# Routed experts on tiles of gathered rows in place of all experts on all tokens, in an attention and mixture-of-experts block

## What is computed

```python
logits = x @ gate_w.T                       # E = 8 experts
_, idx = top_k(logits + lb_bias, 2)         # two experts for each token
w = sigmoid(logits at idx); w = w / (sum(w) + 1e-06)
hidden = square(relu(einsum('nd,ehd->neh', xf, w1)))      # all experts
expert_out = einsum('neh,edh->ned', hidden, w2)
moe_out = einsum('ned,ne->nd', expert_out, we)            # we: w at idx, else 0
shared = square(relu(x @ cfc.T)) @ cproj.T                # the ninth expert, for every token
```

## Time and profile before

| | us |
|---|---|
| median of 3 runs | 986.68 (985.34 to 988.23) |
| the profiled execution, its own time | 985.46 |
| its span | 983.7 |
| busy: PE, DVE, ACT, POOL | 830.8, 768.8, 634.3, 503.7 |
| mean granted clock of PE, share of full speed | 0.943 |

### The profile page before, as it was taken

The page is one execution under the profiler, slowest core; times in us unless marked ns, Lnnn a source line. Parts: engine busy times, 40 slices in busy tenths (PEclk is TensorE's granted clock), DMA queues, the critical chain, the costliest instruction groups (busy, mean ns, idle before and its releaser), DMA issues.

```text
span 983.7 us, 14681 instructions
## 1 busy us (share of the span) xinstructions
PE 830.8 (84%) x4960; PEld 686.6 (70%) x4960; DVE 768.8 (78%) x1972; ACT 634.3 (64%) x914; POOL 503.7 (51%) x348
## 2 busy tenths in 40 slices
PE   2250748999998989999999989898999999889998
PEld 1130537777787878777777878787887877767887
DVE  1679687989989898989898998989898979854221
ACT  1565575867687776768676867777686767563221
POOL 3455644656555665646465555666463656523010
PEclk9765558999999999999999999999999999999999
DMA  7100001010201001010102020010101010101010
GB/s 242 47 1 14 0 11 48 11 58 1 68 2 54 15 12 58 11 58 13 57 1 69 1 68 1 17 53 12 58 12 58 1 55 1 54 1 54 1 54 11
DMA packets 16182, 33.58 MB, mean 34 GB/s; under 512 B 1980, under 2 KB 12905, under 8 KB 14057
## 3 DMA queue, kind: packets, MB, share of 16 engines
q1 hardware_dynamic: 13760, 27.61, 9.0%
q0 software_dynamic: 1248, 4.73, 1.4%
q10 hardware_dynamic: 1096, 0.29, 0.2%
HBM read 28.30 MB, written 4.33 MB: 33 GB/s over the span
## 4 chain that ended last, share of the span: by engine, by line
PE 38%; DVE 33%; issue 11%; ACT 9%; POOL 6%; DMA 2%; ACTq 0%; DVEq 0%; POOLq 0%
PE y_ps L711 12%; PE h_ps L698 8%; PE s_ps L655 6%; DVE fsum L825 5%; PE m_ps L663 5%; ACT signs L448 4%; DVE g L968 4%; DVE fold_a L822 4%; DVE asum L856 4%; PE m_ps L671 3%; DVE first L939 3%; PE m_ps L614 3%; POOL over L306 3%; DVE fold_b L829 2%; ACT hid L494 2%
## 5 line engine op out<-in xcount | busy, mean ns | idle before, releaser
L306 POOL TENSOR_TENSOR over<-S,tau 128x1232 f32<-128x1232 f32 x128 | 285.8, 2248 | 189.1 <-DVE tau L841 186.4
L711 PE MATMUL y_ps<-w_sb,hid 128*128 128x256 f32 x1152 | 281.2, 388 | 47.1 <-ACT hid L494 42.7
L711 PEld LDWEIGHTS y_ps<-w_sb,hid 128*128 128x128 f32 x1152 | 214.4, 191 | 94.2 <-ACT hid L494 63.7
L698 PE MATMUL h_ps<-x1nT,w_sb 128*128 128x256 f32 x1152 | 277.3, 385 | 0.0
L698 PEld LDWEIGHTS h_ps<-x1nT,w_sb 128*128 128x128 f32 x1152 | 216.7, 192 | 30.0 <-issue 3.0
L825 DVE TENSOR_REDUCE fsum<-over 128x16 f32<-128x1232 f32 x128 | 183.2, 1431 | 27.9 <-ACT over L450 27.9
L448 ACT ACTIVATE signs<-over 128x1232 bf16<-128x1232 f32 x128 | 156.1, 1220 | 14.7 <-POOL over L306 14.7
L450 ACT ACTIVATE over<-over 128x1232 f32<-128x1232 f32 x128 | 157.5, 1231 | 4.1
L822 DVE TENSOR_TENSOR fold_a<-signs 128x640 bf16<-128x640 bf16 x128 | 99.4, 777 | 63.5 <-ACT signs L448 63.5
L494 ACT ACTIVATE hid<-g 128x512 f32<-128x512 f32 x144 | 89.8, 624 | 89.0 <-DVE g L968 88.5
L968 DVE SCALAR_TENSOR_TENSOR g<-h_ps,sw_all 128x512 f32<-128x512 f32 x128 | 87.4, 684 | 55.4 <-PE h_ps L698 39.6
(11 more groups left out here) (93 smaller groups left out, 934.4 us busy)
## 6 DMA issues: line engine op xcount, KB each, us to landing
sw_all<-sw_scratch SPq DMA_DIRECT2D x16, 1024.0 KB, 5.2
x_sb<-in_x SPq DMA_DIRECT2D x16, 256.0 KB, 2.6
w_sb<-in_w POOLq DMA_DIRECT2D x2, 2048.0 KB, 12.0
out_y<-y SPq DMA_DIRECT2D x16, 256.0 KB, 5.5
ctx_sb<-in_ctx SPq DMA_DIRECT2D x16, 77.0 KB
wk_sb<-in_wk SPq DMA_DIRECT2D x1, 256.0 KB
wv_sb<-in_wv SPq DMA_DIRECT2D x1, 256.0 KB
wq_sb<-in_wq SPq DMA_DIRECT2D x1, 256.0 KB
```

Of the source, the lines that this page charges most:

```text
L306: return pool.tensor_tensor(dst, S[:, p, t], tau[:, p, t].rearrange("p (h o) -> p h o", o=1).broadcast_to([P, NH, NK]), ALU.subtract)
L698: last = pe.matmul(h_ps[:, i % 2, c, :], w1_sb[:, e, k, c * P:(c + 1) * P], x1nT[:, p, k, :], start=(k == 0), stop=(k == KC - 1))
L711: last = pe.matmul(y_ps[:, t, :], hid[:, i % 2, c, t * P:(t + 1) * P], w2_sb[:, e, c, :], start=(i == 0 and t == 0 and c == 0), stop=(i == ...
```

## The change

The routed experts no longer run on all tokens. The batches form five groups (GROUPS, of 2, 4, 4, 4 and 2 batches). Every token row, with its weight in column 256, is written twice (once for each of its experts) into a DRAM scratch that is ordered by expert; when a group is complete, the scratch is read in tiles of 128 rows, each of one expert. A group has room for 4 tiles a batch and 7 more: 15, 23, 23, 23 and 15, in all 99 tiles, whatever the routing is. The shared expert stays with its batch, as 2 units of 128 rows each. The units of a turn (`Plan`) are:

| turn | 3, 4 | 5-7 | 8 | 9-11 | 12 | 13-15 | 16 | 17, 18 | 19 |
|---|---|---|---|---|---|---|---|---|---|
| shared + routed | 2+0 | 2+4 | 2+3 | 2+6 | 2+5 | 2+6 | 2+5 | 2+9 | 0+20 |

Turn 19 is new. The steps by engine:

- **PE**: a unit is 4 matmuls with 128 columns (`layer1`), 2 with 256 (`layer2`), and for a routed tile 2 transposes ahead (`turned_rows`). `old_rank` counts, with small matmuls against a triangle of ones, how many rows each expert has had before; it stands behind l1(0). The transpose of the roots is gone. h_ps has one buffer where it had two.
- **DVE**: `hidden` rectifies 128x256 of a unit, `shared_added` adds a shared unit's y to x1. `old_slots` turns the ranks into row numbers, and at a group's end `table` (11 small instructions) makes each tile's expert and first row. `gates(0)`, the verdict and `old_slots` stand ahead of Newton round 1 now. `late_gate` has 4 copies and 4 comparisons where it had 1 conversion, 2 comparisons and 2 combined ones.
- **ACT**: for a unit, the copy of the transposed rows, the square, and a weighted copy of y to ys. At the start it clears all four scratches (9216 rows each, two with 1056 bytes a row and two with 1024, 38.3 MB) by DMAs from a zeroed tile.
- **POOL**: the power of the weights is gone. `old_scatter` issues 4 indirect DMAs a batch, between Newton round 3 and round 0; `gather` fetches a batch's rows and adds them to x1 during the DMA, 2 for the first expert at that same place, 2 for the second at the end of the turn. Turns 9, 10, 13 to 16 have one batch of gathers, 17 and 18 two, and batches 10 to 15 are gathered after the last turn.
- **SP**: for each routed tile a register load and a store of ys, then two register loads and two loads for the tile four later (135 KB of rows, 512 KB of weights, into 4 buffers). The copy of x1n to a second buffer takes the place of the spreading of weights.

```diff
+GROUPS = (2, 4, 4, 4, 2)
+FIRST_TURN = (5, 9, 13, 17, 19)
+QUOTA = (4, 6, 6, 9, 15)
+XW = 264
+XB = 4
+YB = 3
...
+def tiles_of(group):
+return 2 * group * T + E - 1
...
+slots = [[("shared", b - 3, t) for t in range(T)] if 3 <= b < nb + 3 else [] for b in range(turns)]
+for g, n in enumerate(GROUPS):
+    b, placed = FIRST_TURN[g], 0
+    for j in range(tiles_of(n)):
+        if placed == QUOTA[g] and b + 1 < turns:
+            b, placed = b + 1, 0
+        slots[b].append(("routed", self.tile_first[g] + j, 0))
+        placed += 1
...
+    def copy_rows(m):
+        sp.wait_ge(x1n_ready.sem, x1n_ready.at(m))
+        if m:
+            sp.wait_ge(xs_scattered[m - 1], 16 * 2 * T)
+        sp.dma_start(x1w[:, 1, :, 0:D], x1w[:, 0, :, 0:D]).then_inc(x1n_copied.sem, 16)
+    def load_tile(r):
+        g, j = plan.routed[r]
+        sp.wait_ge(ys_taken.sem, ys_taken.at(r - XB))
+        sp.wait_ge(table_ready.sem, table_ready.at(g))
+        for f in range(plan.first[g], plan.last[g] + 1):
+            sp.wait_ge(xs_scattered[f], 16 * 2 * T)
+        sp.wait_ge(scratch_cleared, 16 * 4)
+        row0 = sp.value_load(tile_row[0:1, g % 2, j:j + 1], min_val=0, max_val=rows[g] - P)
+        sp.dma_start(xs[:, r % XB], xs_dram[g % 2][bass.ds(row0, P), :]).then_inc(xs_loaded[r % XB], 16)
+        e = sp.value_load(tile_expert[0:1, g % 2, j:j + 1], min_val=0, max_val=E)
+        sp.dma_start(w_tile[:, r % XB].rearrange("p l k n -> p (l k n)"),
+                     w12[bass.ds(e, 1)].rearrange("a p l k n -> p (a l k n)")
+                     ).then_inc(w_loaded[r % XB], 16)
+    def store_tile(r):
+        g, j = plan.routed[r]
+        sp.wait_ge(ys_taken.sem, ys_taken.at(r))
+        if g >= 2 and j == 0:
+            for f in range(plan.first[g - 2], plan.last[g - 2] + 1):
+                sp.wait_ge(gathered[f], 16 * 2 * T)
+        row0 = sp.value_load(tile_row[0:1, g % 2, j:j + 1], min_val=0, max_val=rows[g] - P)
+        sp.dma_start(ys_dram[g % 2][bass.ds(row0, P), :], ys[:, r % YB]).then_inc(ys_stored[r % YB], 16)
...
+    loaded = [0]
+    def load_tiles(last, b):
+        while loaded[0] <= last and loaded[0] < len(plan.routed) and FIRST_TURN[plan.routed[loaded[0]][0]] <= b:
+            load_tile(loaded[0])
+            loaded[0] += 1
+    def turn(b, p, q, ctx=False, new=False, late=False):
         if ctx:
             load_context(b + 1)
+        if b:
+            for f in plan.gathers[b - 1]:
+                store(f)
+        for n in plan.of_turn[b]:
+            kind, r, _ = plan.units[n]
+            if kind == "routed":
+                store_tile(r)
+                load_tiles(r + XB, b)
         if new:
             load_x(b + 2, p)
         if late:
+            copy_rows(b - 2)
+        load_tiles(plan.stored_by[b] + XB, b + 1)
...
+    def old_scatter(f):
+        pool.wait_ge(slots_ready.sem, slots_ready.at(f))
+        pool.wait_ge(x1n_ready.sem, x1n_ready.at(f))
+        pool.wait_ge(x1n_copied.sem, x1n_copied.at(f))
+        pool.wait_ge(w_ready.sem, w_ready.at(f))
+        g = plan.group[f]
+        if f == plan.first[g]:
+            pool.wait_ge(scratch_cleared, 16 * 4)
+            if g >= 2:
+                pool.wait_ge(ys_taken.sem, ys_taken.at(plan.tile_first[g - 1] - 1))
+        for c in range(2):
+            for t in range(T):
+                pool.indirect_dma_start(xs_dram[g % 2],
+                                        bass.IndirectOffsetOnAxis(slot_of[:, f, t, c:c + 1], 0),
+                                        x1w[:, c, t, :], None).then_inc(xs_scattered[f], 16)
+    def stores_of(g, i):
+        return sum(r % YB == i for r in range(plan.tile_first[g + 1]))
+    def gather(f, c):
+        g = plan.group[f]
+        if c:
+            pool.wait_ge(gathered[f], 16 * T)
+        else:
+            pool.wait_ge(base_done.sem, base_done.at(f))
+            for i in range(YB):
+                pool.wait_ge(ys_stored[i], 16 * stores_of(g, i))
+        for t in range(T):
+            pool.indirect_dma_start(x1[:, f, t, :], None, ys_dram[g % 2],
+                                    bass.IndirectOffsetOnAxis(slot_of[:, f, t, c:c + 1], 0),
+                                    compute_op=ALU.add).then_inc(gathered[f], 16)
...
+        if old:
+            old_scatter(b - 3)
+        for f in plan.gathers[b]:
+            gather(f, 0)
...
+    for scratch in (*xs_dram, *ys_dram):
+        lines, width = scratch.shape
+        per = lines // P
+        n = max(n for n in range(1, XB * 4 * D // width + 1) if per % n == 0)
+        act.dma_start(scratch.rearrange("(p a n) w -> p a (n w)", p=P, n=n),
+                      w_tile[:].rearrange("p b l k n -> p (b l k n)")[:, 0:n * width].rearrange(
+                          "p (o s) -> p o s", o=1).broadcast_to([P, per // n, n * width])
+                      ).then_inc(scratch_cleared, 16)
...
+    def rows_turned(n):
+        kind, r, _ = plan.units[n]
+        if kind == "routed":
+            act.wait_ge(xsT_done.sem, xsT_done.at(r))
+            if r >= 2:
+                act.wait_ge(l1_done.sem, l1_done.at(plan.at_routed[r - 2]))
+            act.activation(xsT[:, r % 2], xt_ps, ACT.Copy).then_inc(xsT_taken.sem, 1)
+    def squared(n):
+        act.wait_ge(rectified_ready.sem, rectified_ready.at(n))
+        act.wait_ge(l2_done.sem, l2_done.at(n - 2))
+        act.activation(hid[:, n % 2], rectified[:, n % 2], ACT.Square).then_inc(hid_ready.sem, 1)
+    def rows_weighted(n):
+        kind, r, _ = plan.units[n]
+        if kind == "routed":
+            act.wait_ge(l2_done.sem, l2_done.at(n))
+            if r >= YB:
+                act.wait_ge(ys_stored[r % YB], 16 * (r // YB))
+            act.activation(ys[:, r % YB], y_ps[:, 0:D], ACT.Copy, scale=xs[:, r % XB, D:D + 1]
+                           ).then_inc(ys_taken.sem, 1)
...
+        def step(i):
+            if i == 0 and work:
+                rows_turned(work[0])
+            if i + 1 < len(work):
+                rows_turned(work[i + 1])
+            if i < len(work):
+                squared(work[i])
+            if 1 <= i < len(work) + 1:
+                rows_weighted(work[i - 1])
...
+    def old_rank(f):
+        pe.wait_ge(gate_chain.sem, gate_chain.at(f, 7))
+        pe.wait_ge(xsT_taken.sem, xsT_taken.at(plan.rows_before[f + 3]))
+        pe.wait_ge(slots_ready.sem, slots_ready.at(f - 1))
+        pe.wait_ge(base_ready.sem, base_ready.at(f - 1))
+        g = plan.group[f]
+        base = limits[0:1, g, :, 0] if f == plan.first[g] else base_row[0:1, f % 2]
+        for t in range(T):
+            pe.matmul(rank_ps[:, t], before[:], chosen[:, t], start=True, stop=False)
+            if t:
+                pe.matmul(rank_ps[:, t], ones_bf[:], chosen[:, 0], start=False, stop=False)
+            pe.matmul(rank_ps[:, t], ones_row[:], base, start=False, stop=True)
+        for t in range(T):
+            last = pe.matmul(total_ps, ones_bf[:, 0:1], chosen[:, t], start=(t == 0), stop=(t == T - 1))
+        last.then_inc(rank_done.sem, 1)
...
+    def turned_rows(n):
+        kind, r, _ = plan.units[n]
+        if kind == "routed":
+            pe.wait_ge(xs_loaded[r % XB], 16 * (r // XB + 1))
+            pe.wait_ge(xsT_taken.sem, xsT_taken.at(r - 1))
+            f = plan.ranked_before[n]
+            pe.wait_ge(slots_chain.sem, slots_chain.at(f, 1))
+            pe.wait_ge(base_ready.sem, base_ready.at(f))
+            pe.wait_ge(count_taken.sem, count_taken.at(min(f + 1, NB - 1)))
+            for k in range(KC):
+                last = pe.transpose(xt_ps[:, k], xs[:, r % XB, k * P:(k + 1) * P], ident[:])
+            last.then_inc(xsT_done.sem, 1)
+    def layer1(n):
+        kind, i, t = plan.units[n]
+        if kind == "shared":
+            pe.wait_ge(w_ffn, 16 * 2)
+            pe.wait_ge(x1T_taken.sem, x1T_taken.at(i))
+            w, rhs = ws_sb[:, 0], x1nT[:, i % 2, :, t * P:(t + 1) * P]
+        else:
+            pe.wait_ge(w_loaded[i % XB], 16 * (i // XB + 1))
+            pe.wait_ge(xsT_taken.sem, xsT_taken.at(i))
+            w, rhs = w_tile[:, i % XB, 0], xsT[:, i % 2]
+        pe.wait_ge(rectified_ready.sem, rectified_ready.at(n - 1))
         for c in range(KC):
             for k in range(KC):
+                last = pe.matmul(hid_ps[:, c], w[:, k, c * P:(c + 1) * P], rhs[:, k, :],
                                  start=(k == 0), stop=(k == KC - 1))
         last.then_inc(l1_done.sem, 1)
+    def layer2(n):
+        kind, i, t = plan.units[n]
+        w = ws_sb[:, 1] if kind == "shared" else w_tile[:, i % XB, 1]
+        pe.wait_ge(hid_ready.sem, hid_ready.at(n))
+        y_slot_free(pe, n)
+        for c in range(KC):
+            last = pe.matmul(y_ps[:, 0:D], hid[:, n % 2, c], w[:, c, :], start=(c == 0), stop=(c == KC - 1))
...
+        for t in range(T):
+            for c in range(2):
+                last = dve.tensor_copy(best_f[:, t, c:c + 1], best_at[:, t, c:c + 1])
+        last.then_inc(gate_chain.sem, 1)
```

(31 more changed lines are left out.)

398 lines of the change are left out of this document (220 added, 178 removed).

## The result

The changed kernel takes **1210.84 us**, median of 4 runs (1208.26 to 1216.42), against 987.45 (985.34 to 988.71) before: a ratio of 1.2275, 95% interval 1.2252 to 1.2298. The prediction was 1037, with a range of 950 to 1090. Slower was right; the size was not: 223 us slower instead of 50. The profiled execution has a span of 1211.4 us where the one of before has 983.7, so 227.7 us are to be found.

A forecast was written before the change was run, and what follows sets the result against it. PE and DVE were taken to share the bound, then DVE's list to bind; 58 us given back before turn 18 against 109 lost after it gave a span of 1035, plus 1.8, 1037 us; range 950 to 1090.

The forecast's parts named there:

- step 3: Turns 3 to 14: 606 us in place of 644; with turn 3 at 53.4, -38 us.
- 35 us busy at 1.0, hidden behind DVE: PE in turn 9: loses 31.1 us of work and gains 15.9, so 35 us busy at clock 1.0.
- the clock falls: Rival, turns 5 to 16: PE's 35 us become 50 or more, turns stay near 53.7, total 1078 us; chance 0.14.
- only 0.8 of the scatters' 5.2 goes through: POOL's four scatters ahead of round 0's subtraction: 5.2 us a turn, 0.8 left after a later idle time of 4.39.
- step 1: Start: three more ACT issues of 0.47 us (+1.4), and fewer POOL issues ahead of the first norm (-3.3): -2 us.
- the clearing is late: Rival: below 250 GB/s the clearing ends late and POOL's wait holds the Newton rounds; 1075 us, chance 0.07.
- step 2: Turn 2: PE no longer idles 8.07 us before the roots' transposes, the Newton chain keeps some: -5 us.
- steps 4 and 5: Turn 15 at 51 us: -3; turns 16 and 17 at 43 and 40 instead of 93.6 together: -10.
- step 6: Turns 18 and 19 and the end: 29 tiles at 4.3 us, 125, then 20.6 for the end: +109 us.
- p: Pace of a tile in turns 18 and 19, where nothing else is left: 4.3 us, set by SP's 4.35.
- the loop over SP, landing and transposes: Another bound on a tile's pace: from one tile's ys through loads and transposes to ys two tiles on, 3.95 us each.
- faster: Rival, turns 18 and 19: tile pace at the DMA floor of 2.3 us, total 979 or 948; chance 0.32.

The follow-up runs named there:

- e15: e7 with 60 unread matmuls added on PE in each of turns 2 to 15: 946.94 us.
- e7: The changed kernel without its routed tiles, scatters and gathers, only the shared expert left: 989.56 us.
- e11: The changed kernel without its 64 scatters and the waits on them; tiles and gathers stay: 1199.57 us.
- e6: The changed kernel without its 99 routed tiles; scatters, tables and gathers stay: 1081.86 us.
- e5: The changed kernel with 60 unread matmuls a turn added in three places where PE waits for ACT: 1264.86 us.
- e12: The changed kernel with PE's second scores moved ahead of layer 1 of the turn's fourth unit and its transposes: 1218.48 us.
- e10: The changed kernel with six buffers for a tile's rows and weights instead of four, and a tile's store reusing its load's register: 1185.62 us.
- e1 to e4: Four variants of the changed kernel: clearing from SP, 1225.08 us; scatters ahead of k_diag, 1255.08; 80 unread matmuls a turn, 1261.33; table behind Newton round 1, 1211.95.
- e8: The changed kernel with only xs_scratch cleared from ACT at the start, ys_scratch from SP at the end of its turns 0 and 1: 1211.59 us.
- the control: The changed kernel itself, unchanged, run again on the same chip as e11: 1237.90 us.

## Why the prediction was wrong, and where it was right

*DVE's list and the turns (step 3, the sum's -38 that became +63.5).* The list itself was nearly right: 46.15 us against 46.8 in turn 9, 44.06 against 46.1 in turn 5. `hidden` stayed clear of POOL's subtractions, as expected: 408 to 425 ns in all 131. The step that failed is the next one, "Of the 5.95 us in which DVE idles in turn 9, I take 3 as lasting". (46.1 and 3 are 49.1, not 49.4; that is nothing beside the rest.) It set a turn to the busy time of one engine plus a guess, while a turn is a loop of waits round POOL, ACT, DVE and PE, in which each waits for the one before. DVE idled 15 us of turn 5 and 13 of turn 9, and not 3.

The runs show what a turn is made of. With nothing but attention and the shared expert, and PE kept busy (e15, clock 0.90), the turns 5 to 8 still take 52.1 us on average, 51.3 without a table. That is 1.6 us less than a turn of before, so there was little to win by taking PE's work away. On it come, from the runs: 3.0 us for the clock (e7 less e15, one chip), 4.1 for the tiles (e11 less e7, two chips), nothing to 2 for the scatters (2.2 in e6 less e7, where ACT idles).

By the way it is built the sum 52.1 + 3.0 + 4.1 is the 59.3 of e11; what it is held against is the 59.1 of the changed kernel. The 3.0 are measured where the clock was 0.69. With tiles it is 0.79 in turn 5, and no run shows the clock's part there alone, since in e5 the added matmuls cost more than they gave. e12 shows on one chip 2.2 us a turn for the second scores behind the transposes, about half of the tiles' part.

*PE: "35 us busy at 1.0, hidden behind DVE".* PE was busy 43.13 us at 0.85. The rival *the clock falls* named this mix and had 0.14; even it was too mild, since it let "the turns stay near 53.7", as if PE's stretch could only use up its own slack. Its argument against itself, "a slow PE has no idle time", is what the windows refute: PE idles 16 us of turn 9 and is slow. Here the sentence that was right (an idle stretch is followed by a slow one) should have had the weight.

*POOL.* An indirect DMA was taken at 1.3 us, from bounds of 0.7 and 2.8. Scatters come 1.27 apart, gathers 1.85. That only 0.8 of the scatters' 5.2 goes through was about right where ACT doesn't idle (nothing in e11), though not for the 4.39 us that it counted on: without scatters POOL idles 7.68 us there in the changed kernel (e11), and with them 2.33 in the same turn. By the lists, what it waits for goes back to PE's product of attention.

*The start (step 1).* "three more ACT issues of 0.47" priced a large DMA's issue by small ones. Two of the four held ACT for 37.62 us. The rival *the clearing is late* looked at when it ends, and asked nothing about who stands behind the issue. Its rate of 349 was low, too; the clearing ran at 420 GB/s.

*Turn 2 (step 2).* -2.7 for -5: the 8.07 us before the roots' transposes went, as said. The clock stayed at 0.59 and kept part of it; with PE filled (e5) the turn takes 50.7, -6.

*Turns 15 to 17 (steps 4 and 5).* +13 for -13. Turn 15 takes about 61 us, from POOL's first pair to that of turn 16, where 51 were charged. "Four of them loaded ahead" did not hold: SP's list has turn 16's stores and the copy of x1n ahead of these loads, and they are issued at 1006.83 to 1015.83 us. The first ys of the group comes at 1022.90 and the other eight 4.34 us apart, about the pace of the last two turns. How much the late loads cost isn't separated: PE's waits for the first three tiles are 0.5 to 0.8 us each.

*Turns 18 and 19, and the end (step 6).* +117.6 for +109. p was 4.42 for 4.3, and that was luck in part. SP, which was to set it, needs 3.53 and not 4.35 (a register load about 0.8 and an issue 0.35, not 1.0 and 0.45), and it waits in turn 19, where the prediction had it never idle. The later bound was then the loop over SP, landing and transposes, which had been put at 3.95; the rows of a tile land after 2.0 to 4.9 us there, and the clock is 0.85. e10, which loosens that loop, goes to 3.45, in agreement with this, though it takes a load off SP as well. The end took 25.7 us for 20.6, since eight gathers take 14.5 and were priced 10.8.

*What would show it.* PE's busy time was to be 560 and was 763.5; PEclk of 0.9 was to be kept and was 0.5 to 0.8 in most slices; k_diag was to come 49 to 51 us apart and came 59 apart. The last names the broken step, the first two name the clock. The text also says that the forecast is wrong "if the turns come to 53 or more", and that applies. One slip in the rival *faster*, without effect here: 51 / 29 below 4.3 is 2.5, not 2.6.

## What to carry to other kernels

Before work is taken off a busy engine, ask how long the loop of waits takes with that work gone: the longest busy time is only a lower bound for a turn. Here the loop stood 6.5 us above it even with PE filled (51.29 against DVE's 44.80 in e15) and 15 above it in turn 5 of the changed kernel. Those 51.29 us are hardly below the 53.7 of before. An engine may do what is left at a lower clock once work is taken off it (0.69 in e7 where before had 1.00), so price what is left at the lower level first. And a large DMA belongs to an engine that has nothing behind its issue, and behind the small loads that others wait for.

## What the runs showed of the hardware that was not expected

Useless work made a kernel faster: e7 with 60 more matmuls in each of 14 turns went from 989.56 to 946.94 us, and the granted clock of turn 9 from 0.69 to 0.90.

How long an issue holds its engine is not set by the bytes alone. The same 38.3 MB held ACT 37.62 us as 3072 packets and 16.71 us as 1792 larger ones (the queue's totals, 4380 and 3100, have the small start-up loads in them). Two arrays of the four, 1536 packets, held it 1.34 us. How much the queue takes in is not worked out.

The changed kernel's time depends on the chip (1210.84, 1237.90 and 1244.72 us) where before's does not (984 to 988). In the changed kernel's own profile and e1 to e4, each PE product of attention is followed by ACT's copy at once. In every profiled run on the other chips that scatters, ACT idles 2.3 to 6.1 us there once a turn (11 to 14 times), until within 1.6 us of the end of a scatter or gather, and the trace names no instruction of the core that released it. A row of e8 in turn 9, then POOL's rows of the same stretch:

```profile
538.16 0.38 ACT L654 ACTIVATE OT<-m_ps 128x256 f32<-128x256 f32 x1 [6.14 <-remote]
```

```profile
529.52 1.09 POOL L493 DMA_INDIRECT xs_scratch<-x1w,slot_of  x1 [0.16 <-issue]
...
536.64 1.57 POOL L509 DMA_INDIRECT x<-ys_scratch,slot_of  x1 [0.31 <-issue]
```

It is absent in e7 and e15 (no indirect DMAs) and in e11 (gathers alone). e6 and e8 have it on the chip of e7, and the control has it on the chip of e11. So it goes with the scatters, by single runs of kernels that lack them and the waits on them; what it waits for, and why the chips of the first profile and of e1 to e4 are without it, stays open.
